# Last four units of the attention: the last query's low part and one split of turned weights put ahead of sums and exponentials, residual rows loaded two steps later

## The reference

```
x = x + attention(layernorm(x), ctx)          # 32 query heads, 8 key/value heads, D = 128
    q, k = rope(q), rope(k); p = softmax(where(mask, q k^T / sqrt(D), -1e9)); (p v) Wo
x = x + layernorm(x) @ dequantize(qweight, qzeros, scales) + bias
```

## Time and profile before

| | |
|---|---|
| time, median of 3 runs | 2247.34 us (2245.83 to 2247.9) |
| the profiled execution's own time | 2246.71 us |
| its span (first to last instruction) | 2244.9 us |
| PE busy | 2218.7 us, 99% |
| DVE, ACT, POOL busy | 61%, 47%, 62% |
| granted TensorE clock, share of full | 0.999 |

### The profile page before, as it was taken

One profiled execution on the slowest core, in us unless ns is written; L12 is line 12 of the kernel. 1 busy time (PEld: TensorE's weight loads), 2 busy tenths in 40 slices (PEclk: granted clock), 3 DMA queues, 4 the chain that ended last, 5 costly groups with the idle time before them and its releaser, 6 DMA issues.

```text
span 2244.9 us, 33169 instructions
## 1 busy us (share of the span) xinstructions
PE 2218.7 (99%) x10562; PEld 1863.0 (83%) x10562; DVE 1372.3 (61%) x2536; ACT 1053.2 (47%) x2296; POOL 1393.5 (62%) x980
## 2 busy tenths in 40 slices
PE   8999999999999999999999999899999999999999
PEld 6888888888888888888888888778888888888887
DVE  4782575777777778877777777523675445453532
ACT  3132123767666667666666666622333333331100
POOL 1320553788888889888888888765663354354210
PEclk9999999999999999999999999999999999999999
DMA  7766675688787889888888888688554464451111
GB/s 258 265 228 217 241 264 197 210 254 244 239 262 236 245 252 272 247 262 237 242 250 247 241 250 243 205 312 265 198 187 153 161 198 151 158 194 69 47 47 47
DMA packets 299899, 476.71 MB, mean 212 GB/s; under 512 B 23568, under 2 KB 195888, under 8 KB 299824
## 3 DMA queue, kind: packets, MB, share of 16 engines
q1 hardware_dynamic: 285744, 440.12, 62.7%
q10 hardware_dynamic: 13312, 33.56, 3.8%
q0 software_dynamic: 768, 2.10, 0.3%
HBM read 303.70 MB, written 171.98 MB: 212 GB/s over the span
## 4 chain that ended last, share of the span: by engine, by line
PE 89%; DVE 5%; POOL 3%; issue 1%; ACT 1%; DMA 1%; SPq 0%; ACTq 0%; DVEq 0%; POOLq 0%
PE ps L241 21%; PE ps L242 21%; PE ps L243 21%; PE ps L814 9%; PE ps L816 8%; PE ps L815 8%; POOL s_buf L1560 1%; PE ps L838 1%; ACT wq_t L882 1%; POOL rope_tmp L1560 1%; DVE rope_tmp L1171 0%; DVE rope_tmp L1170 0%; DVE rope_tmp L1169 0%; DVE wq_t L1160 0%; DVE act_t L1232 0%
## 5 line engine op out<-in xcount | busy, mean ns | idle before, releaser
L241 PE MATMUL ps<-act_t,wq_t 128*128 128x512 f32 x1280 | 500.4, 391 | 3.7 <-DVE act_t L1232 2.6
L242 PE MATMUL ps<-act_t,wq_t 128*128 128x512 f32 x1280 | 499.8, 390 | 0.0
L243 PE MATMUL ps<-act_t,wq_t 128*128 128x512 f32 x1280 | 498.2, 389 | 0.0
L1633 POOL TENSOR_TENSOR b_parts<-wraw,b_parts 128x512 fp32r<-128x512 f32 x112 | 199.1, 1778 | 260.3 <-ACT b_parts L1032 260.3
L814 PE MATMUL ps<-b_parts,a_parts 128*128 128x512 f32 x896 | 349.1, 390 | 1.8 <-POOL b_parts L1633 1.5
L816 PE MATMUL ps<-b_parts,a_parts 128*128 128x512 f32 x896 | 348.6, 389 | 0.0
L815 PE MATMUL ps<-b_parts,a_parts 128*128 128x512 f32 x896 | 348.6, 389 | 0.0
L1339 DVE TENSOR_TENSOR a_parts<-xring,a_parts 128x1024 fp32r<-128x1024 f32 x112 | 147.5, 1317 | 305.1 <-ACT a_parts L1027 305.1
L1615 POOL TENSOR_TENSOR q_t<-pt_raw,q_t 128x1024 fp32r<-128x1024 f32 x124 | 302.6, 2441 | 41.0 <-ACT q_t L1010 38.2
L1560 POOL TENSOR_TENSOR rope_tmp<-rope_tmp 128x512 f32<-128x512 f32 x144 | 193.5, 1343 | 185.8 <-DVE rope_tmp L1171 184.9
L1027 ACT ACTIVATE a_parts<-xring 128x1024 fp32r<-128x1024 f32 x112 | 118.7, 1060 | 390.2 <-PE ps L816 382.0
(11 more groups left out here) (132 smaller groups left out, 4367.2 us busy)
## 6 DMA issues: line engine op xcount, KB each, us to landing
sq_scratch<-scores SPq DMA_DIRECT2D x124, 512.0 KB, 3.0
pt_raw<-sq_scratch SPq DMA_DIRECT2D x496, 128.0 KB, 4.1
xring<-left_scratch SPq DMA_DIRECT2D x112, 512.0 KB, 3.8
left_scratch<-s_buf SPq DMA_DIRECT2D x64, 640.0 KB, 5.3
wraw<-in_L_xattn_Wq SPq DMA_DIRECT2D x64, 512.0 KB
wraw<-in_L_xattn_Wo SPq DMA_DIRECT2D x64, 512.0 KB, 4.5
v_scratch<-kv_t ACTq DMA_DIRECT2D x32, 512.0 KB, 3.3
k_scratch<-kv_t ACTq DMA_DIRECT2D x32, 512.0 KB, 4.9
```

The lines of the kernel that those rows point to most:

```text
L241: eng.matmul(dst, lh, rh, start=(k == first), stop=False)
L242: eng.matmul(dst, lh, rl, start=False, stop=False)
L243: mm = eng.matmul(dst, ll, rh, start=False, stop=(k == last))
L1633: pool.tensor_tensor(b_parts[:, s % 2, 1, :], wraw[s % 2][:, 0:NW], b_parts[:, s % 2, 0, :].bitcast(F32), ALU.subtract).then_inc(right_lo, 1)
```

## The change

Four edits, three of them in unit 4 of the last group. The work of every engine is the same instructions as before; only their order changes, and on PE and DVE not even that.

```diff
 # ScalarE, attention(last=True)
                     if last and u8 == 4:
                         step_hi(0)
+                        turned_hi(G, 3)
                     if not (last and u8 >= 5):
                         ...
                         query_hi(...)
                     ...
                         exponents(nG, nxt)
                     ...
-                    if last and u8 <= 4 or not last:
+                    if not tail:
                         if u8 > 0:
                             turned_hi(G, u8 - 1, first=first and u8 < 3)

 # GpSimd, attention(last=True)
-                    if not (last and u8 >= 6):
+                    if not (last and u8 >= 5):
                         if u8 >= 2:
                             turned_lo(G, u8 - 2)
                     ...
                         rope_sum(rope_tmp, q_rot, G * UPG + (u8 + 4), q_sum)
+                    if last and u8 == 4:
+
+                        query_lo(TILES[(u8 + 3) % 4], G * UPG + (u8 + 3))
+                        turned_lo(G, 3)
                     qq = (u8 - 4) // 2
                     if not (first and qq < 0):
                         combine(G * 4 + qq, qq % 2, u8 % 2, fresh=first and qq == 0)
-                    if not (last and u8 >= 5):
+                    if not (last and u8 >= 4):
                         query_lo(TILES[(u8 + 3) % 4], G * UPG + (u8 + 3))

 # SyncE, the first loop over steps
-                if s < 20:
-                    r = (s - 4 + 8) % 16
+                if 6 <= s < 22:
+                    r = (s - 6 + 8) % 16
                     sp.dma_start(rows[:, r, :], x_rows[row_tile(r)]).then_inc(rows_in[r // 8], 16)
```

## The result

| | before | after |
|---|---|---|
| time, median of 14 runs each | 2246.06 us (2244.66 to 2247.9) | 2251.39 us (2249.21 to 2254.2) |
| ratio after/before, 95% interval | | 1.0022 (1.0015 to 1.0029) |
| the profiled execution | 2246.71 us | 2252.2 us |
| its span | 2244.9 us | 2250.4 us |
| PE busy | 2218.7 us | 2222.8 us |

The change makes the kernel slower by about 5 us, 0.2%. The forecast was slower by 2; the measured median lies inside the range, near its upper end, and the change itself (+5.3 us by the medians) outside the 1 to 4 us that I had forecast for it. The first surprise is in the fourth and fifth rows: 4.1 of the 5.5 us by which the span grew are PE *busy* time, with the same instructions. My sum had nothing but PE's idle time in it.

The account below looks back on a forecast made before the run. PE, busy 2218.7 of 2244.9 us, was taken as the bound, with only its idle time to change. 2246.71 + 2.9 - 0.8 + 0 = 2248.8 us, plus 0.6 for the median: 2249.4 us, range 2246.2 to 2252.2.

Parts of the forecast that it names:

- Part 1: ScalarE, `turned_hi(3)` ahead of the last `query_hi`: it waits for its transfers to land, making `query_hi` 3.1 us late.
- rival of the landing that doesn't bind: Turned weights land by about 1418.3: `weigh(3)` 1.6 us early, `weigh(5)` +0.2 us, median 2246.8 us; chance 0.14.
- Part 2: GpSimd, `query_lo` and `turned_lo(3)` ahead of the sums: sums 60 end 3.8 us late and hold `out_copy(4)`.
- price of +2.9 us for the tail: Delay of `weigh(6)` and step 0 from the new order, bounded by +1.25 and +4.5 us.
- the sum's premise: Whole kernel: a new order changes only PE's idle time; at most 8.5 us (0.4%) can be won.
- Part 3: SyncE, residual rows two steps later: 0.8 us less waiting at steps 7 and 10, nothing at step 22.
- -0.8 us at steps 7 and 10: Gain from the later residual rows, out of 1.5 us of PE's waits there; bounds 0 and 1.5 us.
- 0 at step 22: Cost of residual rows at s = 20 and 21: none, as loads had about 2 us to spare; other end 1.0.
- late loads of step 2: Sums 61 hold step 2's right operand and PE waits: +4.9 us or more, median 2252.3 us; chance 0.13.
- my +2.1: Whole kernel: net forecast change in us, +2.9 for the tail and -0.8 at steps 7 and 10.

Follow-up runs that it names:

- e5: Changed kernel with GpSimd's order as before; ScalarE's move and the later residual rows stay; 2250.11 us, ratio 1.0017 to the kernel before.
- e2: Changed kernel with ScalarE's order as before; GpSimd's new order and the later residual rows stay; 2248.72 us, ratio 1.0012 to the kernel before.
- e6: Changed kernel with `right_summed(1)` and the sums' first part moved ahead of the last `query_lo` on GpSimd; 2249.67 us, ratio 1.0014.
- e1: Changed kernel with 30 spare matmuls on PE in three waits of the tail; 2248.85 us, ratio 1.0015 to the kernel before.
- e9: Changed kernel with 30 spare matmuls in the tail's waits and residual rows back at s = 4 to 19; 2248.49 us, ratio 1.0006.
- e11: Kernel before with 24 spare matmuls in the tail's waits and nothing else; 2245.85 us, ratio 0.9993.
- e3: Changed kernel with residual rows back at s = 4 to 19, the tail's new order kept; 2250.40 us, ratio 1.0014 to the kernel before.
- e4: Kernel before with only the residual rows moved, to s = 6 to 21; 2247.55 us, ratio 1.0012.
- e7: Kernel before with residual rows at s = 6 to 19 and the last two at 24 and 25; 2246.06 us, ratio 0.9999.
- e8: e7 with GpSimd's `query_lo` ahead of the sums, `turned_lo(3)` between their parts, `right_summed(1)` last; 2245.82 us, ratio 0.9999 to the kernel before.
- e10: e8 with 24 spare matmuls in the tail's waits; 2245.15 us, ratio 0.9991 to the kernel before.

## Why the prediction was right, and where it was wrong

**Part 1 held.** ScalarE stood 3.5 us for `pt_raw`, `turned_hi(3)` ran at 1421.13 (I had 1421.05), `query_hi` at 1422.09 (1422.05), `tail_high(4)` at 1424.58 (1424.55). e5 shows that this move alone makes PE's wait of 4.7 us. The rival of the landing that doesn't bind is out in every profile of this order. The 2.0 us plus bytes over 436 GB/s that the prediction takes from the Trainium skill ("DMA: Bandwidth & Descriptors", the section on the anatomy of one DMA) are given there for transfers that GpSimd issues; SP issues these, so the 2.3 us were a rough estimate from the start, and in after the last of the four took 4.7 us.

**Part 2 held for the order.** Scores 6 at 1424.10, the sums 60 at 1432.09 (1432.0), `out_copy(4)` held by them at 1432.23 (1432.1), `weigh(5)` at 1434.33 (1434.3). The contended instruction was L1628 (1.71 us) in after and `right_summed(1)` in e2, the size the same 1.0 us. e6 shows the link by cutting it, though not its price. The price of +2.9 us for the tail is right for the order alone: e1's tail is +2.3 with a landing 0.55 us sooner than after's, together 2.85, and by medians it is 2.6 (e9 against e11). `weigh(3)` came at 1426.83 without a wait where I had 1426.5 with 0.7: scores 6 ran at half clock.

**The failed step is the sum's premise, "all that a new order can win or lose is PE's idle time".** It leaves out what idle time does to the clock. Step 0 began at 1444.23, not near 1441. The tail's +5.84 us are 2.3 of order, 0.55 of a later landing and 3.0 of a clock at half, this last by e1. That is the pair of profiled executions, of which the one before had no fall in the tail. Over many runs the clock costs after 2.5 us (after minus e1; e3 minus e9 is 1.9), but it costs the kernel before too, about 1.6 (before minus e11, in one job). Only the difference, about 0.9 us, is the change's.

**Part 3 was wrong in sign.** I took -0.8 us at steps 7 and 10 and 0 at step 22. The wait of 1.5 us in the earlier trace rows does not go with the rows' place: e3, e9 and e11, with the rows at their old steps, have at most 0.3 us there, and e6, with the late rows, has 1.4. Of thirteen profiles these two have it, and its cause stays open. At step 22 the wait that I had bounded by 1.0 us was 0.60 us in after, 0.33 in e4, 1.7 in e6 and 2.41 in e1, and there was none in e2 and e5, which have the late rows too. The left operand of that step, loaded while the rows and the dense weights pass, took 6.3 us to land before, 8.8 in after and 10.7 in e1 (tile, issuing queue, count, size, us from issue to landing):

```profile
xring<-left_scratch SPq DMA_DIRECT2D x1, 512.0 KB, 6.3
```

```profile
xring<-left_scratch SPq DMA_DIRECT2D x1, 512.0 KB, 8.8
```

```profile
xring<-left_scratch SPq DMA_DIRECT2D x1, 512.0 KB, 10.7
```

Over all profiles this load took 5.7 to 6.3 us with the old rows (four), 7.5 to 10.7 with the two late transfers (six), and 7.6 to 8.6 in e7, e8 and e10, which have neither of them there; e8 even has a wait of 0.37 us. So the 2 us that I estimated to be spare were not always there, and the two transfers are not all of it. By e4 the part costs 1.5 us by medians (ratio 1.0012); that its place is s = 20 and 21 is likely by e7 and not shown. Together: 2.6 for the order, 0.9 for the clock (2.5 that after loses less the 1.6 that before loses) and 1.5 for the rows make 5.0 us against 5.3 measured by medians and 4.9 (3.4 to 6.5) by the ratio; the parts were measured in different jobs and are known to about 1 us each. In the medians, then, most of what my +2.1 missed is part 3, a loss of 1.5 instead of a gain of 0.8, and the clock is the smaller part; in the profiled pair it is the clock.

**The rivals.** The late loads of step 2 did not happen: where there is a wait in front of it, it is 0.25 us (e1, e9). The forecast came out near enough by luck. Its change was +2.1 us and the measured one is +5.3. Its base was 2247.34 us, the median of the three runs shown, where the median of 14 is 2246.06: 1.3 us too high. That, and a range wider than the missing terms, put the time inside.

**What stays open.** In which executions the clock falls, and how often, differs between runs of one kernel; I can only say what stood in front of each fall. In e5 and e6 it fell 1.3 and 0.8 us before the long wait ended; in e7 1.5 us behind a wait of 2.1 us, where the kernel before had the same wait and no fall. Why `pt_raw` lands between 3.1 (e3) and 4.2 us (e5) behind the start of `weigh(2)` in the same order of transfers wasn't settled either, nor the spread of step 22's load.

## What to carry to other kernels

When one engine is full nearly everywhere, a move that gathers its short waits into a longer one can cost more than the sum of waits: price the work behind the wait at half clock as a second end of the range, and look where it lies. In front of another engine's long delay it was free here; in front of PE's own chain a stretch cost 1.4 to 2.1 us. And price the kernel before the same way, since it may lose the clock in some executions too. Before an instruction is moved up, read when its data land, and then follow what is queued behind it on every engine up to the next wait of the full one: here a wait of 3.5 us on ScalarE reached `out_copy(4)` over two other engines. A wait of 1 us in one profiled execution is not a term to be won: the one of the earlier trace rows is in two profiles of thirteen, and one of the two has the very change that was to remove it.

## What the runs showed of the hardware

- The granted clock fell in the tail in seven of the nine profiles whose waits were not filled (all but before and e4), and in none of the four with spare matmuls. 24 to 30 matmuls of about 0.23 us, whose results nobody reads, kept it at full; in the kernel before they brought 1.6 us by medians, less than the interval can vouch for.
- The kernel before, over 95 runs: those with a mean clock of 1.000 have a median of 2245.1 us (24 runs), those with 0.999 of 2246.9 (43), with 0.998 of 2247.0 (24), with 0.997 of 2249.2 (4). So part of what looks like noise of the measurement goes with the clock. The mean does not tell where it fell: before, e3, e10 and e11 each have 3.4 us at half near 909 us, too.
- Beside VectorE's `step_lo` an addition on GpSimd took 1.71 us instead of 0.74 (after) and 2.28 instead of 1.29 (e2), 1.0 us more in both; `step_lo` itself was stretched too, from 1.23 to 2.19 us.
- One and the same load of 512 KB in a busy stretch took 5.7 to 10.7 us to land over the thirteen profiles. With two more transfers of 512 KB in front of it, it took 7.5 us or more; without them it took up to 8.6. The DMA engines' mean share there was 0.79 before.
